# A modulated four-layer convolution on one core: one PSUM read moved ahead of an SBUF step in the blur, one edge read moved behind it, a prologue without filler products, and a last group stored by halves

## What is computed

```python
def _layer(x, style, w, b, mw, mb, typ):
    s = style @ mw.T + mb
    weight = SCALE * w * s[:, None, :, None]
    demod = lax.rsqrt(jnp.sum(weight * weight, axis=(2, 3)) + EPS)
    weight = weight * demod[:, :, None, None]
    if typ == 'same':         out = conv_same(x, weight) + b
    elif typ == 'upsample':   out = blur(conv_up(x, weight) + b, 2 * blur_k, (1, 1))
    elif typ == 'downsample': out = conv_down(blur(x, blur_k, (2, 2)), weight) + b
    return out
for i, typ in enumerate(('same', 'upsample', 'same', 'downsample')):
    out = _layer(out, style, weights[i], biases[i], mod_w[i], mod_b[i], typ)
return x + out
```

## Time and profile before

| | |
|---|---|
| median of 3 runs | 169.03 us (167.65 to 169.82) |
| profiled execution | 167.63 us, of it span 165.6 us |
| PE busy | 147.6 us (89%), 2353 products |
| DVE busy | 113.4 us (68%) |
| ACT busy | 91.6 us (55%) |
| POOL busy | 74.7 us (45%) |
| HBM | 8.91 MB read, 8.39 MB written |

### The profile page before, as it was taken

One profiled execution on the slowest core, in us unless ns is written; L12 is line 12 of the kernel. 1 busy time (PEld: TensorE's weight loads), 2 busy tenths in 40 slices (PEclk: granted clock), 3 DMA queues, 4 the chain that ended last, 5 costly groups with the idle time before them and its releaser, 6 DMA issues.

```text
span 165.6 us, 5479 instructions
## 1 busy us (share of the span) xinstructions
PE 147.6 (89%) x2353; PEld 104.0 (63%) x2353; DVE 113.4 (68%) x183; ACT 91.6 (55%) x181; POOL 74.7 (45%) x98
## 2 busy tenths in 40 slices
PE   7789999999998199989998999899989999969930
PEld 5366896866565047646876667676758765648830
DVE  7758626997779930799189728955992799391460
ACT  3316387447174118384859666857768485833430
POOL 7300039599980196950690096029304920950000
PEclk9965699999999869999999999999999999999996
DMA  4959000051001500007940980295055008206326
GB/s 130 351 137 246 29 4 0 4 199 60 0 4 46 208 6 0 4 0 273 352 143 8 224 279 4 63 236 216 2 114 145 4 0 187 70 4 149 108 55 198
DMA packets 9735, 17.64 MB, mean 107 GB/s; under 512 B 4752, under 2 KB 5360, under 8 KB 9712
## 3 DMA queue, kind: packets, MB, share of 16 engines
q1 hardware_dynamic: 9424, 16.98, 35.3%
q10 hardware_dynamic: 288, 0.33, 0.7%
HBM read 8.91 MB, written 8.39 MB: 105 GB/s over the span
## 4 chain that ended last, share of the span: by engine, by line
PE 60%; DVE 20%; issue 7%; ACT 5%; DMA 3%; ACTq 1%; DVEq 1%
PE p_c L611 22%; PE p_h L593 12%; PE p_k L556 6%; DVE H_sb L1085 5%; PE p_k L542 5%; DVE H_sb L1088 4%; PE p_k L572 3%; DMA w1n<-in_L_cond_weights_dram 3%; DVE w_sb L1078 3%; DVE w_sb L1082 2%; ACT M_sb L839 2%; DVE H_sb L1091 2%; ACT w_sb L839 2%; PE p_h L469 1%; DVE d_sb L1058 1%
## 5 line engine op out<-in xcount | busy, mean ns | idle before, releaser
L1110 DVE TENSOR_TENSOR p_c<-p_c,s_sb 128x1024 f32<-128x1024 f32 x13 | 16.0, 1233 | 25.8 <-PE p_c L611 22.1
L611 PE MATMUL p_c<-dd_sb,Tw 64*64 64x256 f32 (+1 forms) x512 | 28.4, 369 | 0.0
L883 ACT ACTIVATE ot<-p_c,pvec 128x508 f32<-128x508 f32 x26 | 20.5, 863 | 9.1 <-PE p_c L611 9.1
L611 PEld LDWEIGHTS p_c<-dd_sb,Tw 64*64 64x64 f32 x512 | 21.2, 133 | 6.8 <-issue 1.9
L593 PE MATMUL p_h<-H_sb,W_st 64*64 64x448 f32 (+1 forms) x192 | 20.4, 555 | 4.1 <-DVE ze L974 3.8
L243 POOL TENSOR_TENSOR Tw<-Tw,di_sb 128x128 f32<-128x128 f32 x7 | 3.2, 456 | 41.4 <-ACT Tw L848 41.3
L263 POOL TENSOR_TENSOR dx_sb<-xin 128x1032 f32<-128x1032 f32 x8 | 19.8, 2476 | 2.3 <-issue 2.2
L611 PE MATMUL p_c<-d_sb,Tw 64*64 64x256 f32 x320 | 19.8, 386 | 0.0
L611 PE MATMUL p_c<-dx_sb,Tw 64*64 64x256 f32 x320 | 18.9, 375 | 0.0
L1058 DVE TENSOR_TENSOR d_sb<-xin 128x2072 f32<-128x2072 f32 x8 | 18.5, 2309 | 0.0
L1066 DVE TENSOR_TENSOR dd_sb<-d_sb 128x2064 f32<-128x2064 f32 x8 | 18.4, 2301 | 0.0
(11 more groups left out here) (172 smaller groups left out, 258.7 us busy)
## 6 DMA issues: line engine op xcount, KB each, us to landing
xin<-in_x_dram SPq DMA_DIRECT2D x16, 512.0 KB, 5.3
out_dram<-ot SPq DMA_DIRECT2D x14, 512.0 KB, 6.3
out_dram<-ot SPq DMA_DIRECT2D x3, 256.0 KB, 3.6
out_dram<-ot ACTq DMA_DIRECT2D x1, 256.0 KB, 4.5
wn<-in_L_cond_weights_dram SPq DMA_DIRECT2D x1, 192.0 KB, 3.6
mwn<-in_L_cond_mod_w_dram SPq DMA_DIRECT2D x1, 128.0 KB, 2.2
xe<-in_x_dram SPq DMA_DIRECT2D x2, 64.0 KB, 9.1
w1n<-in_L_cond_weights_dram ACTq DMA_DIRECT2D x1, 48.0 KB, 4.8
```

The costliest lines, as they stand in the source:

```text
L611: ins = pe.matmul(bank[j * C:(j + 1) * C, i], Tw[q % NW][rows, blk, j, :], moving(rows, j, n), start=(first and n == 0), stop=(n == len(bl ...
L883: act.activation(ot[q % NO_T][:, i, 4 + par:4 + par + 2 * n - 1:2], bank[:, i, 2:2 + n], ACT.Identity, bias=pcol(W_C, 2 * q + i), scale=pc ...
L1110: dve.tensor_tensor(bank[:].rearrange("p i (n h) -> p i n h", h=2), p_a[:, :, w * NQ:(w + 1) * NQ].unsqueeze(3).to_broadcast([P, 2, NQ, 2] ...
```

## The change

- **Blur.** L1085 takes the other neighbour. The two reads of `p_k` with the factor -64 come next, now into `w_sb`, and signal a new semaphore `M_read`. The sum SBUF to SBUF is last and signals `H_made`. R(q) for q > 2 waits for `M_read` and no longer for `H_made`.
- **ze.** The read of ze moves on DVE from behind dd(1) to behind `blur_M(2)`, ahead of d(1) and dd(1).
- **Prologue.** The two `keep_busy(1)` go. The taps k = 1 move behind the turned sums, the taps k = 2 behind the demodulation. ACT issues the load of `w1n` second and no longer fourth.
- **Last quad.** The wait for `y02_made` 14 moves from a2 to bc2. The seed goes to `p_k` and `p_a`, 256 positions each. ACT makes `s_out` ahead of s. a13 is done in two parts into two banks, bc3 and bc1 by halves in turn, and DVE's sums and outputs follow by halves.

```diff
             def blur_M(q):
...
-                dve.scalar_tensor_tensor(out=H_sb[:], in0=w_sb[:, :, 1:NH + 1], scalar=14.0, in1=w_sb[:, :, 0:NH],
+                dve.scalar_tensor_tensor(out=H_sb[:], in0=w_sb[:, :, 1:NH + 1], scalar=14.0, in1=w_sb[:, :, 2:NH + 2],
                                          op0=ALU.mult, op1=ALU.add).then_inc(blurred, 1)
-                dve.wait_ge(blurred, n + 5)
-                dve.tensor_tensor(H_sb[:], H_sb[:], w_sb[:, :, 2:NH + 2], ALU.add).then_inc(blurred_twice, 1)
-                dve.wait_ge(blurred_twice, q - 1)
                 for i in range(2):
-                    ins = dve.scalar_tensor_tensor(out=H_sb[:, i, 2:5], in0=odd[i], scalar=pcol(W_A64, 2 * q + i),
-                                                   in1=H_sb[:, i, 2:5], op0=ALU.mult, op1=ALU.add)
-                ins.then_inc(H_made, 1)
+                    dve.wait_ge(blurred, n + 5)
+                    dve.scalar_tensor_tensor(out=w_sb[:, i, 2:5], in0=odd[i], scalar=pcol(W_A64, 2 * q + i),
+                                             in1=w_sb[:, i, 2:5], op0=ALU.mult, op1=ALU.add).then_inc(M_read, 1)
+                dve.wait_ge(M_read, 2 * (q - 1))
+                dve.tensor_tensor(H_sb[:], H_sb[:], w_sb[:, :, 0:NH], ALU.add).then_inc(H_made, 1)
             def compose_R(q, bank):
...
-                    pe.wait_ge(H_made, q - 2)
+                    pe.wait_ge(M_read, 2 * (q - 2))
             for q in range(QUADS):            # DVE
                 if q > 0:
                     make_dd(q)
-                if q == 1:
-                    scale_edge("ze", one_after_the_other, ze[:], V_E2, WZ)
...
                 if q == 0:
+                    scale_edge("ze", one_after_the_other, ze[:], V_E2, WZ)
                     make_d(1)
             # PE, prologue
             blurred_taps(p_h[:, 0], p_y[:, 0], 0)
-            blurred_taps(p_h[:, 0], p_y[:, 0], 1)
...
             sums_turned(0)
-            blurred_taps(p_h[:, 0], p_y[:, 0], 2).then_inc(put["FT"], 1)
+            blurred_taps(p_h[:, 0], p_y[:, 0], 1)
...
-            pe.wait_ge(made["bias"], 1)
-            keep_busy(1)
+            blurred_taps(p_h[:, 0], p_y[:, 0], 2).then_inc(put["FT"], 1)
...
             ins.then_inc(put["GT"], 1)
-            keep_busy(1)
             # ACT
             act.dma_start(cn[:], cond).then_inc(cond_loaded, 16)
+            act.dma_start(w1n[C:P], weights[1]).then_inc(w1_loaded, 16)
             act.dma_start(bn[0:LAYERS], mod_b).then_inc(b_loaded, 16)
             act.dma_start(bn[LAYERS:2 * LAYERS], biases).then_inc(b_loaded, 16)
-            act.dma_start(w1n[C:P], weights[1]).then_inc(w1_loaded, 16)
             def seed(q):
...
+                elif q + 1 == QUADS:
+                    for bank in (p_k, p_a):
+                        act.activation(bank[:, :, 0:NQ], bank_a2(q)[:, :, 0:NQ], ACT.Copy).then_inc(seeded, 1)
             def product_a2(q):
...
-                wait(pe, y02_made, 2 * q)
+                wait(pe, y02_made, 2 * q if q + 1 < QUADS else 0)
+            def last_products():
+                q = QUADS - 1
+                pe.wait_ge(d_made, q + 1)
+                pe.wait_ge(seeded, 2 * q)
+                pe.wait_ge(T_sums, 3 * QUADS)
+                part(q, half(p_k, 0), (B_U + 1, B_U + 3), odd(q, 1), first=False).then_inc(a13_done, 1)
+                part(q, half(p_a, 0), (B_U, B_U + 2, 0), odd(q, 0), first=False).then_inc(a13_done, 1)
+                pe.wait_ge(dd_made, q + 1)
+                for h in range(2):
+                    of = slice(h * NQ // 2, (h + 1) * NQ // 2)
+                    if h == 1:
+                        pe.wait_ge(e1_made, q + 2)
+                    bank = bank_y13(h)[:, :, 0:NQ]
+                    part(q, parity(bank, 0), (7, 3), second(q, 1, 0, of))
+                    part(q, parity(bank, 1), (5, 1), second(q, 1, 1, of), first=False).then_inc(bc3_done, 1)
+                    if h == 0:
+                        pe.wait_ge(e1_made, q + 1)
+                    else:
+                        pe.wait_ge(e_scaled, 2 + 2 * 2)
+                    bank = bank_y02(h)[:, :, h * NQ:(h + 1) * NQ]
+                    part(q, parity(bank, 0), (8, 4, 0), second(q, 0, 0, of), first=False)
+                    part(q, parity(bank, 1), (6, 2), second(q, 0, 1, of), first=False).then_inc(bc1_done, 1)
             def last_outputs():
...
+                scaled_e(q, p_k, 0, slice(0, m))
+                unscaled_e(0)
+                unscaled_e(1)
+                scaled_e(q, p_k, m, slice(m, NQ))
+                outputs(0)
+                outputs(1)
```

More of the change, by code:

```diff
@@ L231, in bank_bc3 @@
         def bank_bc3(q):
-            return p_a if not alone(q) else p_k if q + 2 == QUADS else p_h
+            return p_k if alone(q) else p_a
         def add_ident(eng, q):
@@ L464, in blurred_halves @@
                 return ins
-            def keep_busy(times):
-                for _ in range(times):
-                    pe.matmul(p_h[:, 1, 0:256], pe_warm[:, 0:P], pe_warm[:], start=True, stop=True)
             pe.wait_ge(warm_made, 1)
-            keep_busy(4)
+            for _ in range(4):
+                pe.matmul(p_h[:, 1, 0:256], pe_warm[:, 0:P], pe_warm[:], start=True, stop=True)
             pe.wait_ge(ident_made, 1)
@@ L643, in product_a13 @@
                 pe.wait_ge(T_sums, 3 * (q + 1))
[L645 to L651, removed]
-                pe.wait_ge(dd_made, q + 1)
[L653 to L660, removed]
+                part(q, half(p_a, 0), (B_U, B_U + 2, 0), odd(q, 0), first=(q == 0))
@@ new lines, in product_a13, with second, product_bc1 @@
+                part(q, half(p_a, 1), (B_U + 1, B_U + 3), odd(q, 1), first=False).then_inc(a13_done, 1)
+            def second(q, of, s, half=slice(0, NQ)):
+                return lambda rows, j, n: dd_sb[rows, j, of, s, n + half.start:n + half.stop]
+            def product_bc1(q):
+                pe.wait_ge(dd_made, q + 1)
+                pe.wait_ge(e1_made, q + 1)
+                part(q, parity(p_b, 0), (8, 4, 0), second(q, 0, 0), first=False)
+                part(q, parity(p_b, 1), (6, 2), second(q, 0, 1), first=False).then_inc(bc1_done, 1)
@@ L662, in product_bc3 @@
             def product_bc3(q):
-                last = alone(q)
                 pe.wait_ge(dd_made, q + 1)
-                if not last:
+                if alone(q):
+                    pe.wait_ge(T_evac, 4 * QUADS)
+                else:
                     pe.wait_ge(e3_made, q + 1)
[L668 to L673, removed]
@@ L767, in _ @@
                     product_bc3(q)
[L768 to L772, removed]
+                product_bc1(q)
                 if not alone(q):
@@ L1112, in make_e, with scaled_e @@
                                   s_sb[:], ALU.add).then_inc(signal, 1)
-            def scaled_e(q):
-                dve.wait_ge(s_scaled, 2 * (q - QUADS + 3))
-                wait(dve, y13_made, 2 * q if q + 1 == QUADS else 0)
+            def scaled_e(q, bank, first, half=slice(0, NQ)):
                 for i in range(2):
-                    dve.scalar_tensor_tensor(out=e_out[:, i], in0=p_a[:, i, NQ:2 * NQ].unsqueeze(2).to_broadcast([P, NQ, 2]),
-                                             scalar=pcol(W_D3, 2 * q + i), in1=s_out[:, i], op0=ALU.mult, op1=ALU.add)\
+                    n = half.stop - half.start
+                    dve.scalar_tensor_tensor(out=e_out[:, i, half],
+                                             in0=bank[:, i, first:first + n].unsqueeze(2).to_broadcast([P, n, 2]),
+                                             scalar=pcol(W_D3, 2 * q + i), in1=s_out[:, i, half], op0=ALU.mult, op1=ALU.add)\
                         .then_inc(e_scaled, 1)
@@ L1134, in last_outputs, with unscaled_e, outputs @@
             def last_outputs():
-                q, n = QUADS - 1, NQ - 2
+                q, n, m = QUADS - 1, NQ - 2, NQ // 2
+                def unscaled_e(h):
+                    dve.wait_ge(a13_done, q + 2)
+                    dve.wait_ge(s_made, 2 * QUADS)
+                    dve.tensor_tensor(bank_y02(h)[:, :, h * NQ:(h + 1) * NQ].rearrange("p i (n h) -> p i n h", h=2),
+                                      p_a[:, :, h * m:(h + 1) * m].unsqueeze(3).to_broadcast([P, 2, m, 2]),
+                                      s_sb[:, :, h * m:(h + 1) * m], ALU.add).then_inc(e1_made, 1)
+                def outputs(h):
+                    dve.wait_ge(bc3_done, QUADS + h)
+                    wait(dve, stored[q % NO_T], 32 * (q // NO_T))
+                    first = 2 if h == 0 else 0
+                    for i in range(2):
+                        dve.wait_ge(e_scaled, 2 + 2 * h + i + 1)
+                        at = 5 + h * 2 * n
+                        dve.scalar_tensor_tensor(out=ot[q % NO_T][:, i, at:at + 2 * n - 1:2],
+                                                 in0=bank_y13(h)[:, i, first:first + n], scalar=pcol(W_D3, 2 * q + i),
```

(2 more changed lines are left out.)

48 lines of the change are left out of this document (22 added, 26 removed).

## The result

The kernel after takes 157.32 us (median of 4 runs, 156.48 to 157.89), the kernel before 169.43 (4 runs, 167.65 to 170.55): ratio 0.931, 95% interval 0.922 to 0.941. Medians are of all runs, and each ratio compares only the runs of either kernel within about 1.5% of its fastest one. The forecast was 158.0, the range 155.6 to 160.8. The profiled execution took 156.48, of it span 154.4: 11.2 us less than the span before.

The account below looks back on a forecast made before the run. The loop was taken as almost bound by PE, with one large hole ahead of T(2). Terms 5.6 + 1.9 + 1.2 + 1.7 = 10.4 us gave 157.2 or 158.6; forecast 158.0, range 155.6 to 160.8.

Parts of the forecast that it names:

- ze, 5.6: Ahead of T(2): earlier read of ze starts T(2) 4.1 us sooner and keeps full clock, 1.5 more; bounds 4.1 to 5.8.
- Rival (b): Quad 1: DVE and POOL stand in each other's way, costing 0 to 1 us; 158.6 us, chance 0.08.
- Start 4 us earlier too: On POOL: the offset of ze and the sums of quad 2 start 4 us earlier, following ze's earlier read.
- Blur, 1.9: Ahead of R in four places after R(3): earlier `M_read` removes PE's idle time, 1.9 us; bounds 1.2 to 2.2.
- 2.2 - 0.28: Blur: PE's idle time ahead of R in five places, less R(3)'s, already counted under ze: 1.9 us.
- Prologue, 1.2: Up to `compose_H`: without two zero products and with biases read earlier, it starts at 19.5, not 20.70; bounds -0.8 to 2.9.
- if the clock rises at 19.5 again: Prologue: R(0) and R(1) both run at half clock until 19.5, so `compose_H` starts then: 1.2 us gained.
- Last quad, 1.7: End of the kernel: last store issued 0.8 us earlier and landing 0.9 faster, 3.6 against 4.5; bounds 0.6 to 2.6.
- (a): Prologue: the clock rises late, as PE's work gets sparser by two dense products; price 2.0, 160.0 us, chance 0.12.
- (c): Blur: the new order doesn't release R and T, so the 1.9 us stay; 160.0 us, chance 0.06.
- (d): Slower than before: the clock stays at 1.2 GHz far beyond 19.5; 172.4 us if until about 43; chance 0.02.
- (e): More than summed: full clock from R(0) on and faster landing of stores; 156.0 us, chance 0.07.

Follow-up runs that it names:

- late edges: Kernel after with GpSimd's last edge steps and first two copies of edges moved from the end of quad 1 to that of quad 2: 156.83 us, ratio 0.926.
- late edges with `xe`: Kernel after with those GpSimd edge steps and copies at the end of quad 2, and the sum of the bias to `xe` too: 157.14 us, ratio 0.943.
- taps back: Kernel after with the order of the taps and of ACT's loads as before, the two zero products still out: 158.42 us, ratio 0.934.

## Why the prediction was right, and where its terms were off

- **ze, 5.6: measured 5.8.** T(2) started behind R(3) and ran at full clock, as said. Not foreseen was what it sets off later, 0.8 to 1.4 us. Rival (b) had the mechanism, at the wrong place: d(1), dd(1) and d(2) did not hold PE up; POOL's own steps were delayed by them, and its differences for quads 2 and 3 slid into the blurs of quads 3 and 4. "Start 4 us earlier too" is the step: ze's offset did, and lost half of it, and the sum to `xe` lost the rest. The two variants that move edge steps bear out the last part: with each a hold in the blur went, in the second one to another step.
- **Blur, 1.9: worth 2.7 alone, 1.3 in the kernel after.** Two errors of opposite sign. The term "2.2 - 0.28" counts idle time; a wait also costs the 0.24 of overlap. And the hold took 1.0 to 1.4, with a wait of 0.56 ahead of R(5) where none was to be. The new quad of 14.73 is under the 15.0 that I named.
- **Prologue, 1.2: measured 3.2, above the bound of 2.9.** The step that failed is "if the clock rises at 19.5 again": it rose at 16.0, and R(1) ran at full clock. In the seven profiles that record it the rise came 1.7 to 4.7 us after R(0)'s start, between 16.0 and 22.2, so it goes with the work more than with the time; why it comes where it does isn't shown. R(0) started 3 us earlier than before, and 0.8 before my 15.1, since the second group of taps was hidden. The bound was too low, too: at full clock `compose_H` comes 2.3 after R(0)'s start (13.51 to 15.83 with the idle places filled), 17.4 in my sum and not 17.8. And 2.12 is the time of 21 records of R(0), not of 24; all 24 took 2.32. How much of the 3.2 the edit gives isn't settled: over all profiles its prologue started `compose_H` 1.6 to 3.8 before the two with fillers at half clock, and 0.5 to 2.3 after the one at full clock.
- **The fillers and the Trainium skill.** The Trainium skill's page "TensorE: Matmul & The Clock Gate", section "Why this matters for your kernels", asks for warm-up products in advance, for measuring, so that what follows is not taken at the lower clock. My reading of the rows, that the two fillers do not keep the clock up, held in two of three profiles with them (both still at half clock in R(0)). In the third, of the blur's order alone, R(0) took 1.14 for 21 records and the fillers 0.70 each. By cost they lost 2.3. Two fillers in idle places went with full clock in both profiles with them, and all ten runs lie within 153.5 to 155.2, so here the advice paid where the products cost no time.
- **Last quad, 1.7: measured 0.9.** ACT's issue came 1.1 earlier (0.8 forecast). The step that failed is the landing, "With half of the bytes still to move I take 3.6": the other half was still moving, it took 4.5, and even without the first two stores 3.9. The sum also followed ACT's store alone. SP's third landed later in both kernels, and it was issued only 0.7 earlier, behind a second issue of 1.41.
- **Rivals.** (a) price and mechanism did not come in the kernel after; (c) and (d) did not come. (e) came by half: the prologue was faster than summed, the landing was not. The total of 10.4 (11.2 by the spans) is right partly by luck: the prologue's surplus of 2.0, which another execution need not repeat, covered the 1.4 that the blur and the last quad lacked.

## What to carry to other kernels

Price a wait by its idle time plus the overlap that the waiting group loses. When a step on a shared engine is moved forward, follow the other engines' work behind it until the next place where both touch SBUF: what was won here was partly given back 15 to 30 us later. Fill PE's idle places, not its path, if the clock is to stay up, and don't take a clock change to come again at the time at which one profile showed it.

## What the runs showed of the hardware that I had not expected

- The prologue's clock differs between executions of one prologue: `compose_H` moved by 1.8 us with that of the kernel after, by 3.8 with the old one (16.86 and 20.70). In four profiles (R waiting for `H_made`, late edges, late edges with `xe`, taps back) the granted clock is recorded as 1.00 throughout the prologue, though R(0) took 2.12 for 21 records or 2.20 for 24, as in the rows at 1.2 GHz, and R(1) 2.08 to 2.28. Durations tell the clock there, the record doesn't. A window of the late-edges kernel during R(0):

```profile
16.00:17.00 1.00, 1.00 (x17) 1.00 (x14) 0.91 (x5) 0.12 (x1) 0.00 (x0) 1.00 0.74 291
```

- A POOL step of two SBUF inputs holds a DVE step of two SBUF inputs by up to 1.8 us (2.92 against 1.09), and DVE's hold POOL's (3.02 became 4.97); DVE's steps with one input in PSUM pass (0.74 for two, in all profiles). The Trainium skill, "SBUF — State Buffer", section "SBUF: two separate sides", says that whichever starts first has the shared ports for the whole instruction and the other blocks; the rows agree (the held steps end 0.94 to 0.96 after POOL's, about one step of 1.09).
- Stores of 256 KB issued 1.5 us apart slow each other: 4.5 us to land for each of the last two, 3.9 and 3.2 without the first two.
- The issue of a store on SP's queue can take longer than the usual 0.60: the second of the last quad took 0.73 to 1.55 in ten profiles, and the one behind it waited.
